# The row of the MLP's bias and second weight moves from attention's first stage into the last dense stage's table

## The reference, cut to what matters

```python
h = jnp.maximum(_layernorm(x, axis=-1), 0.0)
x = x + _L1_gnn_ref(h, ...)          # two convolutions: the dense stages before attention
h = jnp.maximum(_layernorm(x, axis=-1), 0.0)
x = x + _L2_gnn_ref(h, ...)          # attention:
#   head_out = relu(num / safe_den);  concat = head_out.reshape(N, -1)
#   hidden = relu(concat @ mlp_W1 + mlp_b1)
#   return hidden @ mlp_W2 + mlp_b2
h = jnp.maximum(_layernorm(x, axis=-1), 0.0)
x = x + _L3_gnn_ref(h, edge_index)
```

## Time and profile before

| | us |
|---|---|
| median of 3 runs | 5505.44 |
| the three runs | 5505.36, 5505.44, 5557.91 |
| the profiled execution | 5495.54 |
| its span, first to last instruction | 5493.7 |
| mean granted TensorE clock | 0.827 |

### The profile page before, as it was taken

One profiled execution on the slowest core, in us unless ns is written; L12 is line 12 of the kernel. 1 busy time (PEld: TensorE's weight loads), 2 busy tenths in 40 slices (PEclk: granted clock), 3 DMA queues, 4 the chain that ended last, 5 costly groups with the idle time before them and its releaser, 6 DMA issues. The chain is left out here.

```text
span 5493.7 us, 65636 instructions
## 1 busy us (share of the span) xinstructions
PE 3499.6 (64%) x13792; PEld 1856.5 (34%) x13792; DVE 3590.7 (65%) x10139; ACT 2632.4 (48%) x7510; POOL 3069.8 (56%) x2834
## 2 busy tenths in 40 slices
PE   1112177442888959899799958868846548973332
PEld 0111133221333326566243334545521114543232
DVE  2223299892444569889577679979967877863232
ACT  1222299792444527667355525657745644540000
POOL 3777677686565428787433125568875510017766
PEclk9999999555999979999899979966766768985555
DMA  7233377794333239767222169957758856652222
GB/s 260 80 89 87 107 252 250 301 407 139 106 107 105 91 116 316 250 182 202 83 78 82 53 206 315 312 186 234 238 169 263 276 187 192 227 183 91 82 90 60
DMA packets 670756, 968.71 MB, mean 176 GB/s; under 512 B 120003, under 2 KB 304356, under 8 KB 668512
## 3 DMA queue, kind: packets, MB, share of 16 engines
q1 hardware_dynamic: 604576, 852.07, 46.7%
q0 software_dynamic: 65856, 113.13, 8.0%
HBM read 614.83 MB, written 355.85 MB: 177 GB/s over the span
## 5 line engine op out<-in xcount | busy, mean ns | idle before, releaser
L953 DVE TENSOR_TENSOR conv_logits_leaky<-conv_logits_z,conv_logits_sloped 128x512 f32<-128x512 f32 x784 | 529.1, 688 | 299.1 <-issue 181.6
L896 ACT ACTIVATE conv_logits_sloped<-conv_logits_z 128x512 f32<-128x512 f32 x784 | 455.0, 600 | 351.8 <-PE conv_logits_z L868 97.8
L861 PE MATMUL conv_logits_z<-conv_logits_hdT,conv_logits_wsum 128*128 128x512 f32 x784 | 395.9, 649 | 107.2 <-DVE conv_logits_leaky L953 68.3
L1214 PE MATMUL conv_aggregate_part<-conv_aggregate_weighed,conv_wlc 128*128 128x512 f32 x784 | 363.1, 605 | 50.8 <-DVE conv_aggregate_weighed L1296 50.8
L868 PE MATMUL conv_logits_z<-diffT,conv_logits_wl 128*128 128x512 f32 x784 | 360.2, 601 | 43.7 <-issue 31.2
L160 POOL DMA_INDIRECT conv_logits_hs<-H,idx x196 | 187.1, 955 | 268.7 <-PE conv_logits_hsT_ps L854 219.5
L1455 PEld LDWEIGHTS conv_nodes_o_ps<-conv_wmean,conv_nodes_hT 128*128 128x128 f32 x1568 | 229.4, 225 | 251.9 <-DVE conv_nodes_hT L1476 154.3
L1296 DVE TENSOR_TENSOR conv_aggregate_weighed<-conv_aggregate_alpha,diffT 128x512 f32<-128x512 f32 x392 | 310.3, 851 | 6.4 <-DMA conv_aggregate_alpha<-ALPHA 6.4
L1455 PE MATMUL conv_nodes_o_ps<-conv_wmean,conv_nodes_hT 128*128 128x128 f32 x1568 | 272.4, 326 | 64.4 <-DVE conv_nodes_hT L1476 63.9
L1521 ACT ACTIVATE conv_nodes_squares<-conv_nodes_o_ps 128x128 f32<-128x128 f32 x784 | 205.5, 276 | 188.5 <-PE conv_nodes_o_ps L1455 186.8
L166 POOL DMA_INDIRECT AGG<-gine_edges_rows,gine_edges_idx x196 | 207.6, 1059 | 142.2 <-issue 100.9
(11 more groups left out here) (279 smaller groups left out, 10233.4 us busy)
## 6 DMA issues: line engine op xcount, KB each, us to landing
conv_aggregate_alpha<-ALPHA SPq DMA_DIRECT2D x392, 256.0 KB
HX<-gine_finish_hx SPq DMA_DIRECT2D x98, 512.0 KB
AGG<-gine_edges_zero SPq DMA_DIRECT2D x14, 1792.0 KB
gine_mlp_x<-x SPq DMA_DIRECT2D x98, 256.0 KB
gine_mlp_agg<-AGG SPq DMA_DIRECT2D x98, 256.0 KB
YT<-gine_mlp_yT SPq DMA_DIRECT2D x98, 256.0 KB
gine_finish_x<-x SPq DMA_DIRECT2D x98, 256.0 KB
gine_finish_yT<-YT SPq DMA_DIRECT2D x98, 256.0 KB
```

Of the source, the lines that this page charges most:

```text
L861: pe.matmul(z[h][:, :], wsum[:, h * D:(h + 1) * D], hdT[j % 3][:, :], start=True, stop=True).then_inc(z_done[0], 1)
L896: act.activation(sloped[H * c + h][:, :], z[h][:, :], ACT.Copy, scale=SLOPE).then_inc(sloped_made[c], 1)
L953: dve.tensor_tensor(leaky[H * c + h][:, :], z[h][:, :], sloped[H * c + h][:, :], ALU.max).then_inc(leaky_made[c], 1)
L1214: last = pe.matmul(part[n % 2][:, :], g.wlc[:, h * D:(h + 1) * D], weighed[n % 2][:, h, :], start=(h == 0), stop=(h == H - 1))
```

## The change

The dense stage now also reads w2 and b1, makes the same row (relu, product in a PSUM buffer of the stage) and adds it into its table b2, so that X2 holds x plus the whole row. TensorE and POOL wait for that sum (`b2_made`) before their first tile. gat_logits drops the row's setup and the add of each tile: x3 is loaded from X2, its ring grows from 4 to 6, and the load of tile d waits for the total of tile d-6. h4 and total keep their rings of 4, and SP keeps its order.

```diff
@@ conv_nodes
+        if final:
+            square_ones, b1, relu_b1, w2 = m.sb("square_ones", [P, P]), m.sb("b1", [P, 2]), m.sb("relu_b1", [P, 2, P]), m.sb("w2", [P, 2, D])
...
-        n_weights = 1 + 2 * SUB
+        n_weights = 1 + 2 * SUB + (2 if final else 0)
...
+                if final:
+                    sp.dma_start(w2[:, :, :], g.mw2.rearrange("(j p) n -> p j n", p=P)).then_inc(weights_in, 16)
+                    with nc.allow_non_contiguous_dma("256 biases"):
+                        sp.dma_start(b1[:, :], g.mb1.rearrange("o (j p) -> p (o j)", p=P)).then_inc(weights_in, 16)
...
                 pool.wait_ge(weights_in, 16 * n_weights)
+                if final:
+                    pool.wait_ge(b2_made, SUB)
...
                 pe.wait_ge(bias_step, 3)
+                if final:
+                    pe.wait_ge(relu_made, 2)
+                    for j in range(2):
+                        last = pe.matmul(o_ps[3][:, 0, :], relu_b1[:, j, :], w2[:, j, :], start=(j == 0), stop=(j == 1))
+                    last.then_inc(c_done, 1)
+                    pe.wait_ge(b2_made, SUB)
...
+                if final:
+                    dve.memset(square_ones[:, :], 1.0).then_inc(set_once, 1)
+                    dve.wait_ge(set_once, 2)
+                    for j in range(2):
+                        dve.tensor_scalar(relu_b1[:, j, :], square_ones[:, :], b1[:, j:j + 1], 0.0, ALU.mult, ALU.max).then_inc(relu_made, 1)
+                    dve.wait_ge(c_done, 1)
+                    for a in range(SUB):
+                        dve.tensor_tensor(b2[:, a * D:(a + 1) * D], o_ps[3][:, 0, :], b2[:, a * D:(a + 1) * D], ALU.add).then_inc(b2_made, 1)
@@ gat_logits
-        x, x3, h4, total = (m.sbs(n, [P, SUB, D], n=4) for n in ("x", "x3", "h4", "total"))
+        x3, h4, total = m.sbs("x3", [P, SUB, D], n=6), m.sbs("h4", [P, SUB, D], n=4), m.sbs("total", [P, SUB, D], n=4)
...
-                sp.dma_start(w2[:, :, :], g.mw2.rearrange("(j p) n -> p j n", p=P)).then_inc(weights_in, 16)
-                with nc.allow_non_contiguous_dma("256 biases"):
-                    sp.dma_start(b1[:, :], g.mb1.rearrange("o (j p) -> p (o j)", p=P)).then_inc(weights_in, 16)
                 def load(d):
-                    past(sp, x3_made, d - 3)
-                    sp.dma_start(x[d % 4][:, :, :], node_rows(g.X2, d)).then_inc(x_in[d % 4], 16)
+                    past(sp, total_made, d - 5)
+                    sp.dma_start(x3[d % 6][:, :, :], node_rows(g.X2, d)).then_inc(x_in[d % 6], 16)
...
-                pe.wait_ge(relu_made, 2)
-                for j in range(2):
-                    last = pe.matmul(c_ps[:, :], relu_b1[:, j, :], w2[:, j, :], start=(j == 0), stop=(j == 1))
-                last.then_inc(c_done, 1)
...
-                dve.wait_ge(weights_in, 5 * 16)
-                for j in range(2):
-                    dve.tensor_scalar(relu_b1[:, j, :], ones[:, :], b1[:, j:j + 1], 0.0, ALU.mult, ALU.max).then_inc(relu_made, 1)
+                dve.wait_ge(weights_in, 3 * 16)
...
-                dve.wait_ge(c_done, 1)
-                for a in range(SUB):
-                    dve.tensor_copy(c[:, a * D:(a + 1) * D], c_ps[:, :]).then_inc(c_made, 1)
-                dve.wait_ge(c_made, SUB)
...
-                def add(d):
-                    dve.wait_ge(x_in[d % 4], 16 * (d // 4 + 1))
-                    past(dve, h4_made, d - 3)
-                    past(dve, total_made, d - 3)
-                    dve.tensor_tensor(flat(x3[d % 4]), flat(x[d % 4]), c[:, :], ALU.add).then_inc(x3_made, 1)
-
                 def take_stats(d):
-                    dve.wait_ge(x3_made, d + 1)
-                    norm.take_stats(dve, x3[d % 4], d % 7)
+                    dve.wait_ge(x_in[d % 6], 16 * (d // 6 + 1))
+                    norm.take_stats(dve, x3[d % 6], d % 7)
...
-                dense = [(4, add_h4), (0, add), (1, lambda d: norm.moments(dve, d % 7, d + 1)), (0, take_stats),
+                dense = [(4, add_h4), (1, lambda d: norm.moments(dve, d % 7, d + 1)), (0, take_stats),
                          (2, lambda d: norm.scales(dve, d % 7, d + 1))]
```

More of the change, by code:

```diff
@@ L1351, in conv_nodes @@
         pos = None if final else m.sb("pos", [P, g.NTE, 2, 16], I32)
+        if final:
+            square_ones, b1, relu_b1, w2 = m.sb("square_ones", [P, P]), m.sb("b1", [P, 2]), m.sb("relu_b1", [P, 2, P]), m.sb("w2", [P, 2, D])
+        relu_made, c_done, b2_made = (m.sem(n) for n in ("relu_made", "c_done", "b2_made"))
         x_made, pos_copied = m.sem("x_made"), m.sem("pos_copied")
@@ L1557, in gat_logits @@
     with Phase(nc, "gat_logits_") as m:
-        ident, eps, ones = m.sb("ident", [P, P]), m.sb("eps", [P, 1]), m.sb("ones", [P, P])
+        ident, eps = m.sb("ident", [P, P]), m.sb("eps", [P, 1])
         a_rows, product, wa = m.sb("a_rows", [P, 2, HID]), m.sb("product", [D, 2, HID]), m.sb("wa", [D, 2, H])
-        b1, relu_b1, w2, c = m.sb("b1", [P, 2]), m.sb("relu_b1", [P, 2, P]), m.sb("w2", [P, 2, D]), m.sb("c", [P, TILE])
         hs, hd, hdT = m.sbs("hs", [P, SUB, D]), m.sbs("hd", [P, SUB, D], n=4), m.sbs("hdT", [P, TILE], n=2)
         logit, logit_dst = m.sbs("logit", [H, TILE], n=2), m.sbs("logit_dst", [H, TILE], n=2)
-        x, x3, h4, total = (m.sbs(n, [P, SUB, D], n=4) for n in ("x", "x3", "h4", "total"))
+        x3, h4, total = m.sbs("x3", [P, SUB, D], n=6), m.sbs("h4", [P, SUB, D], n=4), m.sbs("total", [P, SUB, D], n=4)
         hsT_ps, hdT_ps = ([m.ps(f"{n}{j}", [P, TILE]) for j in range(2)] for n in ("hsT_ps", "hdT_ps"))
-        e_ps, d_ps, c_ps = [m.ps(f"e_ps{j}", [H, TILE]) for j in range(2)], m.ps("d_ps", [H, TILE]), m.ps("c_ps", [P, D])
+        e_ps, d_ps = [m.ps(f"e_ps{j}", [H, TILE]) for j in range(2)], m.ps("d_ps", [H, TILE])
         norm = Norm(m, "norm")
@@ L1568, in gat_logits @@
         hd_in = m.sems("hd_in", 4)
[L1569 to L1572, removed]
+        x_in, h4_out, total_out, logit_out, own = m.sems("x_in", 6), m.sems("h4_out", 4), m.sems("total_out", 4), m.sems("logit_out", 2), m.sem("own")
+        cleared, ident_made, weights_in, product_made, weights_made, eps_set = (
+            m.sem(n) for n in ("cleared", "ident_made", "weights_in", "product_made", "weights_made", "eps_set"))
         turned_done, hdT_made, hsT_made, e_done, d_done, logit_dst_made, logit_made = (
             m.sem(n) for n in ("turned_done", "hdT_made", "hsT_made", "e_done", "d_done", "logit_dst_made", "logit_made"))
-        x3_made, h4_made, total_made = (m.sem(n) for n in ("x3_made", "h4_made", "total_made"))
+        h4_made, total_made = m.sem("h4_made"), m.sem("total_made")
         with nc.Block() as block:
@@ L1672, in normalize @@
                     past(act, total_made, d - 3)
-                    norm.apply(act, h4[d % 4], x3[d % 4], d % 7, ACT.Relu).then_inc(h4_made, 1)
+                    norm.apply(act, h4[d % 4], x3[d % 6], d % 7, ACT.Relu).then_inc(h4_made, 1)
                 for t in range(M + 5):
@@ L1682, in _ @@
                 dve.memset(eps[:, :], EPS).then_inc(eps_set, 1)
-                dve.memset(ones[:, :], 1.0).then_inc(ones_set, 1)
-                dve.wait_ge(ones_set, 1)
-                dve.wait_ge(weights_in, 5 * 16)
-                for j in range(2):
-                    dve.tensor_scalar(relu_b1[:, j, :], ones[:, :], b1[:, j:j + 1], 0.0, ALU.mult, ALU.max).then_inc(relu_made, 1)
+                dve.wait_ge(weights_in, 3 * 16)
                 for j in range(2):
@@ L1719, in add_h4 @@
                     past(dve, total_out[d % 4], 16 * (d // 4))
-                    dve.tensor_tensor(flat(total[d % 4]), flat(x3[d % 4]), flat(h4[d % 4]), ALU.add).then_inc(total_made, 1)
-                dense = [(4, add_h4), (0, add), (1, lambda d: norm.moments(dve, d % 7, d + 1)), (0, take_stats),
+                    dve.tensor_tensor(flat(total[d % 4]), flat(x3[d % 6]), flat(h4[d % 4]), ALU.add).then_inc(total_made, 1)
+                dense = [(4, add_h4), (1, lambda d: norm.moments(dve, d % 7, d + 1)), (0, take_stats),
                          (2, lambda d: norm.scales(dve, d % 7, d + 1))]
```

## The result

| | before | after |
|---|---|---|
| median, us (runs) | 5528.99 (4) | 5717.47 (4) |
| lowest to highest, us | 5505.36 to 5557.91 | 5711.39 to 5765.71 |
| span of the profiled execution | 5493.7 | 5763.9 |
| gat_logits, from its start to the next stage's | 429.5 | 637.4 |
| total of tile 3 to total of tile 92, per tile | 3.85 | 6.24 |

The account below looks back on a forecast made before the run. A chain between engines, none full, was taken to bound gat_logits. Loop +159, stage ends -1 and -3, moved setup +4 sum to +159 us on 5505, rounded to 5665 us; range 5590 to 5740.

Parts of the forecast that it names:

- SP's order: In gat_logits, x's load waits two VectorE steps later, so h4's stores behind it do too; 89 tiles held, +159 us.
- The terms: One tile's loop in gat_logits: total 0.67, to SP 0.03, issue 0.38, landing L, hand-over and normalize 0.03 + 1.63: 2.74 + L.
- L: Landing time of h4's store in gat_logits, taken as 2.9 us, between 2.47 and 3.3, giving 5.64 us a tile.
- drained queues: In gat_logits' new loop the same bytes take longer, so queues are otherwise drained: a DMA share of 0.57.
- The ends of the stage: In gat_logits, -3 us ahead of the total of tile 3 and -1 us over the last five tiles.
- The moved setup: In the last dense stage, two DMAs, memset, products, matmuls and adds delay the start by 4 us, bounds 2 and 8.
- Shares: In gat_logits VectorE's share would fall from 84% to about half, the DMA share to about 0.57.
- the out store: In gat_logits it goes 0.47 us behind h4's, and its buffer is needed 1.63 us after h4 landed: never the later.
- A: In gat_logits the store lands late, L over 3.75; at L = 4.5 the kernel takes 5807 us; chance 0.12.
- B: In gat_logits stores don't hold the chain; DMA limits a tile to 3.33 us: -46 us, about 5460; chance 0.04.
- C: No visible change: loop and relief cancel in gat_logits, or only some tiles are held; 5450 to 5560 us; chance 0.04.
- D: In gat_logits the load of x is late instead, issued two steps ahead of the statistics, not four; no time of its own.

Follow-up runs that it names:

- before_late_load: The kernel before, adds kept, with the load of tile d also waiting for the total of tile d-6: 5427.68 us, 1.0396 of before, 6.25 us a tile.
- x3_ring8: The changed kernel with x3 in a ring of 8 instead of 6: 0.9889 of before in group one, 0.9871 in group two, 3.10 us a tile.
- load_behind_stores_same_wait: The changed kernel with SP's wait left in place but the load of x issued behind the two stores: 5618.20 us, 4.80 us a tile.
- group two: The second set of follow-up runs, on a chip of its own, where the kernel before had a median of 5481.58 us.
- stores_first: The changed kernel with SP issuing each turn's stores ahead of its load of x: 5225.77 us, 1.0047 of before, 4.06 us a tile.
- h4_total_ring6: The changed kernel with h4 and total in rings of 6 instead of 4: 5228.07 us, 1.0058 of before, 4.05 us a tile.
- group one: The first set of follow-up runs, on a chip of its own, where the kernel before had a median of 5207.62 us.

## Why the prediction was right, and where a term was off

The prediction was 5665 us, 5590 to 5740, slower with 0.92. The median is 5717, inside the range and 52 above the value. The direction, the place and the loop were as predicted; one term was too small.

**SP's order (the step on which it was decided).** Right. The load is issued 0.03 us after the total has ended, the h4 store 0.38 behind the load, and normalize waits 89 times, as many as the tiles counted, 4 to 92. before_late_load shows that this wait is enough, and x3_ring8 that without it nothing of the slowdown is left.

**The terms.** The loop was put at 2.74 + L. In the timeline of after everything but the landing, 6.24 - 3.43, is 2.81. That is 0.07 more: the terms that the prediction lists make 2.77 and not 2.74, and total and normalize were 0.02 longer each.

**L.** This is the mis-sized term: 2.9 taken, 3.43 measured. It was put between 2.47, a store behind one other at a quiet moment, and the median 3.3 of a burst. The argument that drained queues would make it faster was wrong in its weight. The queues were drained as predicted (a DMA share of 0.54), and the landing still took as long as in conv_nodes at 0.72. What counted is what stands immediately ahead in the burst: with the load of x ahead 3.4, with it behind 2.1 (load_behind_stores_same_wait). The row with the same place behind loads, 3.3 in conv_nodes, was the near one. 0.53 for L and 0.07 for the other terms, times 89, are 53 us: 212.5 against 159, the whole miss of the sum.

The Trainium skill ("DMA: Bandwidth & Descriptors", section "Anatomy of one DMA — SWDGE (gpsimd) path") would have given an estimate of 2.6 us and 5.34 for a tile. With 6.24 measured its fit was further off than the rows. The shortest landings of before_late_load and load_behind_stores_same_wait, 2.0 both, aren't agreement with its fixed part, as the prediction read the same figure in the earlier trace rows: they are whole transfers of 256 KB, for which the fit gives 2.6. So on SP's path the measured landings lie on both sides of it, under it with nothing ahead and over it behind the load of x.

**The ends of the stage.** Startup: -2.9 predicted as -3 (65.1 to 62.2 us from the stage's start to the total of tile 3). Tail: -1.8 (21.7 to 19.9), predicted -1. Both right.

**The moved setup.** +3.0 us to the first transpose (11.19 to 14.19), predicted +4. The issue of the two DMAs was hidden only in small part: VectorE's first wait grew by 0.76 (9.23 in the earlier trace rows to 9.99). The memset, products, matmuls and adds took 3.0, as predicted. What the prediction missed is that TensorE didn't follow VectorE in the kernel before; VectorE had centred the bias by 3612.58, and the first transpose waited for the first node tile:

```profile
3613.33 1.09 PE L1445 MATMUL conv_nodes_turned<-conv_nodes_ident,conv_nodes_h 128*128 128x128 f32 x4 [32.33 <-DMA conv_nodes_x<-HX]
```

So 0.75 of the 3.0 fell into a wait that was there anyway. In the whole stage the setup can't be told: over all kernels here with the row in that stage it takes 455 to 470 us, over those without it 450 to 466. On the chip of the result it got shorter, 465.8 to 458.2; in group two it takes 468 to 470 in the three kernels with the row and 450.2 in the one execution of before. Whether that is the row or the spread of the stage, one execution doesn't tell.

**Shares.** VectorE 41% where about half was predicted, DMA share 0.54 for 0.57: both go with the longer tile. The sentence that the out store is never the later one held in after (one wait, 2.9 us), but not where h4 lands in 2.1.

**The rivals.** A (L over 3.75, 5807 us) did not come: over the 89 tiles L comes to 3.43, and the longest of the landings that the view gives is 3.7. B, faster, needed the stores to be out of the loop; x3_ring8 is that case, and its floor was too high in the prediction. It put 3.33 us a tile, by 3.2 us of transfer and a DMA share of 0.96; the stage reached 0.99 with 3.07 us of transfer, and 3.10. C, no change, is what stores_first and h4_total_ring6 look like: within 1% of before, with the loop opened in part. D never appeared: no wait of the statistics for x, neither in after nor in x3_ring8; x lands at least 6 us before them in both.

## What to carry to other kernels

When a buffer between a load and its last reader is dropped, work out which step of the releasing engine (here VectorE) the load now waits for, and then follow everything that stands behind it in the same in-order queue: here a load that nobody needed early held back stores whose buffers were needed. The ring must be as deep as the lead of the load plus the lag of its last reader plus one (here 3 + 4 + 1 = 8, not 6) for the release to stay where it was; if memory doesn't allow that, the stores would have to come out from behind the wait by more than one turn, which no kernel here tries; by one turn wasn't enough (stores_first). A store whose landing is waited for should be issued ahead of large loads, and after one loop is opened, look for the next ring that hangs on the same queue. And where a view puts a repeated wait down to nothing, compare it with the landing of the buffer's last store.

## What the runs showed that was not expected

- A store's landing depends on what is queued just ahead of it: 256 KB in 2.1 us first in its burst, 3.4 behind a load of the same size, 4.3 in a stage at a DMA share of 0.83 (5.4 at 0.99, in x3_ring8). The share alone doesn't set it: 3.6 in h4_total_ring6 at 0.81.
- Sixteen DMA engines at a share of 0.99 moved 337 and 342 GB/s in x3_ring8 in its two groups; in the earlier trace rows 0.96 stood for 319.
- Stages with gathers differ between chips by more than the change is worth: the first conv_logits takes 683 to 689 us where the result was measured, 681 to 684 in group two, 518 in group one. The stretch from gat_logits' start to the total of tile 3 is 60 to 65 us where the result was measured and in group two, and 30 to 34 in group one, so the standstill at its start, which the prediction couldn't read the earlier trace rows, goes with the chip. Its cause stays open; nothing here was made to find it.
- The first conv_aggregate has two lengths, 314 to 324 and 373 us, in kernels that don't differ in it. Why, no run here tells.
